# Graph attention applied ahead of its weight in a four-layer graph network kernel, with score terms as row sums and a new order on every engine

## The reference

```
h = relu(layernorm(x)); x = x + L0(h)    # 8-head masked attention, w_qkv, w_proj, + layernorm of itself
h = relu(layernorm(x)); x = x + L1(h)    # rel = (h Wq^T)(h Wk^T)^T * adj, rows scaled to norm 1, times h Wv^T
h = relu(layernorm(x)); x = x + L2(h)    # graph attention, below
h = relu(layernorm(x)); x = x + L3(h)    # adj @ h @ w_out + b_out
```

```
hw = h @ W;  s1 = hw @ a1;  s2 = hw @ a2
e = leaky_relu(s1[:, None] + s2[None, :], 0.2) * adj
att = softmax(e);  out = elu(att @ hw + beta * hw)
```

## Time and profile before

| what | value |
|---|---|
| median of 3 runs | 1475.9 us (1473.24 to 1476.55) |
| the profiled execution | 1474.6 us, its span 1472.8 us |
| TensorE (PE) busy | 1438.2 us, 98% |
| VectorE (DVE) busy | 1273.4 us, 86% |
| ScalarE (ACT) busy | 1134.7 us, 77% |
| GpSimd (POOL) busy | 748.4 us, 51% |
| mean granted TensorE clock | 0.995 of full speed |

### The profile page before, as it was taken

How to read it: one execution, slowest core, us unless ns; L and a number is a source line. 1 busy time by engine, 2 the same in 40 slices (tenths; PEclk the granted TensorE clock), 3 DMA queues, 4 the chain that set the end, 5 groups by cost and what they waited for, 6 DMA issues and landing times.

```text
span 1472.8 us, 47814 instructions
## 1 busy us (share of the span) xinstructions
PE 1438.2 (98%) x16136; PEld 1370.3 (93%) x16136; DVE 1273.4 (86%) x5774; ACT 1134.7 (77%) x2884; POOL 748.4 (51%) x1107
## 2 busy tenths in 40 slices
PE   5999999999999999999999999999999999999996
PEld 5899999999999999999999999999999999999985
DVE  4889988988989889889889889889889889889885
ACT  4778878878877877877877778778778788788753
POOL 3455555555555555555555555555555555555452
PEclk9999999999999999999999999999999999999998
DMA  3000000100000000001001000000001001000000
GB/s 111 17 17 23 31 16 30 31 16 31 30 17 31 30 16 31 28 19 31 24 23 30 23 24 30 24 24 31 23 24 30 23 24 30 19 28 31 9 23 30
DMA packets 38113, 39.90 MB, mean 27 GB/s; under 512 B 2416, under 2 KB 37488, under 8 KB 37872
## 3 DMA queue, kind: packets, MB, share of 16 engines
q1 hardware_dynamic: 37872, 36.84, 7.9%
HBM read 20.05 MB, written 16.78 MB: 25 GB/s over the span
## 4 chain that ended last, share of the span: by engine, by line
PE 95%; DVE 1%; ACT 1%; issue 1%; POOL 0%; DMA 0%; SPq 0%; POOLq 0%; ACTq 0%; DVEq 0%
PE bank L314 34%; PE mid L314 15%; PE bank L349 6%; PE mid L358 5%; PE bank L520 5%; PE bank L370 4%; PE mid L458 4%; PE mid L374 4%; PE bank L330 4%; PE mid L488 4%; PE bank L417 4%; PE mid L330 2%; PE mid L349 2%; PE mid L493 1%; PE mid L527 1%
## 5 line engine op out<-in xcount | busy, mean ns | idle before, releaser
L546 ACT ACTIVATE probs<-masked,neg_max 128x128 f32<-128x128 f32 x1024 | 326.3, 395 | 6.3 <-DVE neg_max L716 6.3
L903 POOL TENSOR_TENSOR rstd<-var_eps,minus_half 128x2 f32<-128x2 f32 x320 | 240.9, 753 | 25.5
L716 DVE CUSTOM_DVE_ANT_0 masked<-mid,mask 128x128 f32<-128x128 f32 x1024 | 234.9, 286 | 6.9 <-issue 6.8
L915 POOL TENSOR_TENSOR xb<-x,b_proj_beta 128x512 f32<-128x512 f32 x64 | 81.9, 1279 | 233.9 <-DVE o_res L828 233.9
L901 POOL TENSOR_TENSOR var_eps<-mean_var,eps 128x2 f32<-128x2 f32 x320 | 63.5, 198 | 243.0 <-DVE mean_var L710 242.7
L706 DVE BATCH_NORM_STATS2 stats<-x 128x6 f32<-128x256 f32 x384 | 143.3, 415 | 0.1
L725 DVE TENSOR_SCALAR z<-x,mean_var,rstd 128x256 f32<-128x256 f32 x384 | 134.5, 405 | 7.1 <-POOL rstd L903 6.7
L946 POOL TENSOR_TENSOR h_t_lo<-h_t_full,h_t_hi 128x512 fp32r<-128x512 f32 x64 | 82.0, 1282 | 79.4 <-ACT h_t_hi L629 79.4
L349 PE MATMUL bank<-ident,probs 128*128 128x128 f32 x768 | 117.6, 276 | 4.9 <-ACT probs L546 4.9
L942 POOL TENSOR_TENSOR e_mask<-e_leaky,adj_sb 128x256 f32<-128x256 f32 x64 | 46.8, 731 | 116.2 <-DVE e_leaky L770 116.2
L370 PE MATMUL bank<-probs_t,v 128*32 128x128 f32 x2048 | 104.5, 276 | 0.3 <-issue 0.3
(11 more groups left out here) (156 smaller groups left out, 5725.8 us busy)
## 6 DMA issues: line engine op xcount, KB each, us to landing
x<-in_x SPq DMA_DIRECT2D x64, 256.0 KB, 2.7
out_x<-x SPq DMA_DIRECT2D x64, 256.0 KB, 2.1
w_qkv_sb<-in_w_qkv SPq DMA_DIRECT2D x1, 768.0 KB, 4.4
w_q_sb<-in_w_q SPq DMA_DIRECT2D x1, 256.0 KB, 4.4
w_k_sb<-in_w_k SPq DMA_DIRECT2D x1, 256.0 KB, 4.6
w_v_sb<-in_w_v_t SPq DMA_DIRECT2D x1, 256.0 KB, 5.8
w_proj_sb<-in_w_proj SPq DMA_DIRECT2D x1, 256.0 KB, 6.0
w_gat_x<-in_w_gat SPq DMA_DIRECT2D x1, 256.0 KB, 7.2
```

The costliest lines, as they stand in the source:

```text
L546: last = act.activation(probs[:, r, s], masked[:, r, s], ACT.Exp, scale=-1.0, bias=neg_max[:, r, s:s + 1])
L716: last = dve.tensor_tensor_reduce(out=masked[:, r, s], in0=mid[:, r, s * N:(s + 1) * N], in1=mask[:], scale=1.0, scalar=LARGE, op0=ALU.add ...
L903: pool.tensor_tensor(rstd[:, k], var_eps[:, k], minus_half[:], ALU.pow).then_inc(ln_rstd[k], 1)
```

## The change

Attention is applied to the rows h2 first and the weight after: att (h2 W) = (att h2) W. In detail:
- h2 = relu(rstd * x2 - mean * rstd) is made by ScalarE straight from x2, as h3 is. z2, its four transposes, both halves of h_t2, the 258-column product, its two banks and the copies to `hw` go.
- s1 and s2 are row sums of h2 times the vectors W a1 and W a2 (`wa_rows`, spread over all partitions once, in step 3, by four transposes and a copy), four `tensor_tensor_reduce` a pair on VectorE, each over 256 elements.
- m = h2^T att_t is four f32 matmuls of 128 columns a pair. Its halves are made by ScalarE and VectorE, and u = m W is a product of 12 matmuls of 256 columns. The two f32 matmuls of the old u go.
- The leaky maximum is made by ScalarE (`Prelu` with s1 as the bias) from PSUM, in the place of `e_sum`; VectorE's instruction goes.
- z0 and z1 are made by ScalarE (`Identity` with scale rstd and bias shift) instead of VectorE; three small `shift` instructions a pair are new on VectorE.
- STREAMS becomes 10, banks are assigned anew, and the order of the blocks is new on all engines. q and k change places around the step's edge.
- At the start, the halves of w_qkv are made in three parts, behind x0's moments on VectorE; the fold moves to step 2, with its two loads behind the constants on SP's queue, and its use to step 4.

```diff
-    STREAMS = 8
+    STREAMS = 10
...
+    def wa_rows_made():
+        pe.wait_ge(wa_made, 2 * C)
+        pe.wait_ge(max_ready[0], done(1, 1))
+        for j in range(2):
+            for c in range(C):
+                last = pe.transpose(wa_bank[:, j * D + c * 128:j * D + (c + 1) * 128],
+                                    w_gat_x[:, c, D + j:D + j + 1].to_broadcast([128, 128]), ident[:])
...
-    transposes(z2_bank, z[2]).then_inc(h_t_psum[2], 1)
-    rows([hw0_bank[:, 0:DX], hw1_bank[:, 0:DX]], h_t[2], w_gat_p, 0, DX).then_inc(hw_psum, 1)
-    for b in range(2):
-        last = pe.matmul(u_bank[:, b * D:(b + 1) * D], att_t[:, b], hw[:, b, 0:D], start=True, stop=True)
+    for c in range(C):
+        for b in range(2):
+            last = pe.matmul(m_bank[:, (c * 2 + b) * N:(c * 2 + b + 1) * N], h2[:, b, c * 128:(c + 1) * 128],
+                             att_t[:, b], start=True, stop=True)
+    rows(halves(u_bank), m_t_p, w_gat_p, 0, D).then_inc(u_psum, 1)
...
-    act.activation(flat(h_t[2][0]), z2_bank, ACT.Relu).then_inc(h_hi_ready[2], 1)
-    act.activation(hw[:, b], bank[:, 0:DX], ACT.Copy).then_inc(hw_ready, 1)
-    act.activation(e_sum[:, b], s2_bank[:, b * N:(b + 1) * N], ACT.Identity, bias=hw[:, b, D:D + 1])
+    last = act.activation(h2[:, b], x2[:, i5, b], ACT.Relu, bias=shift[2][:, b:b + 1], scale=rstd[:, 2, b:b + 1])
+    last = act.activation(z[0][:, b], x0[:, i0, b], ACT.Identity, bias=shift[0][:, b:b + 1], scale=rstd[:, 0, b:b + 1])
+    last = act.activation(z[1][:, b], x1[:, i3, b], ACT.Identity, bias=shift[1][:, b:b + 1], scale=rstd[:, 1, b:b + 1])
+    act.activation(flat(m_t_p[0]), m_bank, ACT.Copy).then_inc(m_hi_ready, 1)
+    act.activation(e_leaky[:, b], s2_bank[:, b * N:(b + 1) * N], ACT.Prelu, bias=s12[:, b, 0:1], alpha=ALPHA)
...
-    normalize(1, p3, x1[:, i3])
-    normalize(0, p0, x0[:, i0])
-    normalize(2, p4, x2[:, i4])
-    dve.scalar_tensor_tensor(e_leaky[:], e_sum[:], ALPHA, e_sum[:], ALU.mult, ALU.max)
+    dve.scalar_tensor_tensor(shift[0][:], mean_var[:, 0, :, 0], -1.0, rstd[:, 0], ALU.mult, ALU.mult)\
+       .then_inc(shift_ready[0], 1)
+    last = dve.tensor_tensor_reduce(out=s12_prod[:, b, j], in0=h2[:, b], in1=wa_rows[:, j], scale=1.0, scalar=0.0,
+                                    op0=ALU.mult, op1=ALU.add, accum_out=s12[:, b, j:j + 1])
+    dve.tensor_tensor(flat(m_t_p[1]), m_bank, flat(m_t_p[0]).bitcast(f32), ALU.subtract).then_inc(m_lo_ready, 1)
```

More of the change, by code:

```diff
@@ L435, in step @@
[L435 to L445, removed]
@@ new lines, in step @@
+                if on[4]:
+                    pe.wait_ge(h_lo_ready[1], done(p4))
+                    bank_free(pe, (h1_full_ready, p4, 1), (y_lo_ready, p9, 1))
+                    columns(g_bank, w_qk_p, 0, h_t[1]).then_inc(g_psum, 1)
+                if on[1]:
+                    pe.wait_ge(h_lo_ready[0], done(p1))
+                    bank_free(pe, (x4_ready, p9, 1), (probs_t_ready[0], p2, 1))
+                    rows(halves(v_bank), h_t[0], w_qkv_p, 2 * D, D).then_inc(v0_psum, 1)
+                if on[4]:
+                    pe.wait_ge(h_lo_ready[1], done(p4))
+                    bank_free(pe, (max_ready[0], p1, 1), (x3_ready, p7, 1))
+                    rows(halves(v1_bank), h_t[1], w_v_p, 0, D).then_inc(v1_psum, 1)
@@ L469, in step @@
[L469 to L476, removed]
@@ L490, in step @@
-                if on[3]:
-                    pe.wait_ge(rel_sq_ready, done(p3))
-                    for b in range(2):
-                        last = pe.matmul(rel_bank[:, 256 + b:257 + b], rel_sq[:, b], ones[:, 0:1], start=True, stop=True)
-                    last.then_inc(sum_sq_psum, 1)
-                if on[1]:
-                    pe.wait_ge(probs_ready[1], done(p1))
-                    bank_free(pe, (h_lo_ready[0], p0, 1), (x4_ready, p7, 1), (o_norm_ready, p2, 1))
-                    transpose_probs(1).then_inc(probs_t_psum[1], 1)
@@ L522, in step @@
                     last.then_inc(y_t_psum, 1)
+                if on[2]:
+                    pe.wait_ge(o_lo_ready, done(p2))
+                    bank_free(pe, (o_norm_ready, p2, 1), (probs_t_ready[2], p2, 1))
+                    for b in range(2):
+                        last = product(o_bank[:, b * D:(b + 1) * D], o_t_p, w_proj_p,
+                                       lambda a, c: a[:, b, c], lambda a, c: a[:, c])
+                    last.then_inc(o_psum, 1)
+                if on[1]:
+                    pe.wait_ge(probs_ready[0], done(p1))
+                    bank_free(pe, (v0_ready, p1, 1), (x4_ready, p9, 1))
+                    transpose_probs(0).then_inc(probs_t_psum[0], 1)
@@ new lines, in step @@
+                if on[5]:
+                    pe.wait_ge(s12_ready, done(p5))
+                    bank_free(pe, (max_ready[2], p1, 1), (att_t_ready, p6, 1), (x2_ready, p5, 2))
+                    for b in range(2):
+                        last = pe.transpose(s2_bank[:, b * N:(b + 1) * N], s12[:, b, 1:2].to_broadcast([128, 128]), ident[:])
+                    last.then_inc(s2_psum, 1)
+                if on[6]:
+                    pe.wait_ge(m_lo_ready, done(p6))
+                    bank_free(pe, (v1_ready, p4, 1), (max_ready[0], p1, 1))
+                    rows(halves(u_bank), m_t_p, w_gat_p, 0, D).then_inc(u_psum, 1)
@@ L529, in step @@
-                    last.then_inc(s2_psum, 1)
-            run(pe, step, [(0, fold), (2, next_weights), (4, last_weights)])
+                        last = pe.matmul(rel_bank[:, 256 + b:257 + b], rel_sq[:, b], ones[:, 0:1], start=True, stop=True)
+                    last.then_inc(sum_sq_psum, 1)
+                if on[3]:
+                    if t == 3:
+                        pe.wait_ge(folded_ready, 2)
+                    pe.wait_ge(z_ready[1], done(p3))
+                    bank_free(pe, (y_lo_ready, p8, 1), (g_ready, p4, 1))
+                    transposes(z1_bank, z[1]).then_inc(h_t_psum[1], 1)
@@ new lines, in step @@
+                if on[0]:
+                    pe.wait_ge(h_lo_ready[0], done(p0))
+                    bank_free(pe, (h_lo_ready[0], p0, 1), (max_ready[1], p1, 1))
+                    columns(q_bank, w_qkv_p, 0, h_t[0]).then_inc(q_psum, 1)
+                if on[4]:
+                    pe.wait_ge(v1_ready, done(p4))
+                    pe.wait_ge(rel_ready, done(p4))
+                    bank_free(pe, (e_leaky_ready, p5, 2), (max_ready[2], p1, 1), (att_t_ready, p6, 1))
+                    for b in range(2):
+                        last = pe.matmul(rel_v_bank[:, b * D:(b + 1) * D], rel[:, b], v1[:, b], start=True, stop=True)
+                    last.then_inc(rel_v_psum, 1)
@@ L586, in step @@
-                if on[7]:
-                    act.wait_ge(shift3_ready, done(p7))
-                    wait_before(act, y_t_psum, p7)
-                    for b in range(2):
-                        last = act.activation(h3[:, b], x3_up[:, i7, b], ACT.Relu, bias=shift3[:, b:b + 1],
-                                              scale=rstd[:, 3, b:b + 1])
-                    last.then_inc(h3_ready, 1)
+                    act.wait_ge(h_t_psum[1], done(p4))
+                    wait_before(act, rel_psum, p4)
@@ L655, in step @@
                 if on[5]:
-                    act.wait_ge(att_t_psum, done(p5))
-                    wait_before(act, u_psum, p5)
-                    act.activation(att_t[:].rearrange("p b n -> p (b n)"), att_bank[:, 0:2 * N], ACT.Copy).then_inc(att_t_ready, 1)
+                    act.wait_ge(s2_psum, done(p5))
+                    wait_before(act, e_mask_ready, p5)
+                    for b in range(2):
+                        act.activation(e_leaky[:, b], s2_bank[:, b * N:(b + 1) * N], ACT.Prelu, bias=s12[:, b, 0:1], alpha=ALPHA)\
+                           .then_inc(e_leaky_ready, 1)
                 if on[1]:
@@ L738, in step @@
             def step(t, par, on):
[L739 to L745 removed]
+                p0, p1, p2, p3, p4, p5, p6, p7, p8, p9, p10 = [t - s for s in range(STREAMS + 1)]
@@ new lines, in step @@
+                if on[3]:
+                    dve.wait_ge(xb_ready, done(p3))
+                    dve.wait_ge(o_psum, done(p3))
+                    dve.tensor_tensor(o_res[:], pair_rows(o_bank), xb[:], ALU.add).then_inc(o_res_ready, 1)
+                if on[1]:
+                    relu_lo(0, p1, z0_bank)
+                if on[3]:
+                    dve.wait_ge(o_psum, done(p3))
+                    dve.tensor_tensor(o[:], pair_rows(o_bank), both(b_proj_bc), ALU.add).then_inc(o_ready, 1)
+                    dve.wait_ge(o_ready, done(p3))
+                    moments(LN_O, p3, o)
@@ new lines, in step @@
+                if on[7]:
+                    dve.wait_ge(u_exp_ready, done(p7))
+                    dve.scalar_tensor_tensor(x2_exp[:], u_exp[:], 1.0, x2[:, i7], ALU.min, ALU.add).then_inc(x2_exp_ready, 1)
+                if on[3]:
+                    dve.wait_ge(ln_moments[LN_O], done(p3, 2))
+                    for b in range(2):
```

(3 more changed lines are left out.)

667 lines of the change are left out of this document (339 added, 328 removed).

## The result

The changed kernel takes 1681.1 us (median of 4 runs, 1678.96 to 1682.04) beside 1474.8 us of the kernel before on the same chip. The ratio is 1.140 (95% interval 1.138 to 1.142). Forecast were 1443 us and a range of 1429 to 1466. Two rivals named the right side, ScalarE late for k_t (1487 us) and a table load (1511 us). Both fell short, by 194 and 170 us, and neither named the instruction that waits.

The account below looks back on a forecast made before the run. TensorE was taken to bound the kernel at 22.2 us a pair. Terms of -32 us over 64 pairs, -1.8 at the start and +2 at the end took 1474.6 to 1442.8, say 1443 us; range 1429 to 1466 (8 in 10).

Parts of the forecast that it names:

- ScalarE late for k_t: Rival: ScalarE's in-order queue makes the scores wait for k_t every step, +0.2 us a pair, 1487 us; chance 0.09.
- a table load: Rival: the leaky function is outside ScalarE's loaded table, two loads a pair, +0.6 us a pair, 1511 us; chance 0.03.
- I find no place that must stall, so I cost the new waits at nothing: Claim, from laying the engines' new orders against TensorE's prices, that the new waits between engines add 0 us.
- signs of being wrong: TensorE waits mid-kernel (scores on k_t, u on m_lo, q on h_t's low half), ScalarE above 97%, or heads above 2.1 us.
- It stays covered: VectorE goes from 19.8 to 19.6 us a pair, of a 21.7 us period, so TensorE still covers it.
- ScalarE comes to 20.2 of 21.7: ScalarE's work per pair rises from 17.7 to 20.2 us, leaving 1.5 us of slack in the 21.7 us period.
- The sum on TensorE: TensorE's change per pair: -0.44 - 0.03 + 0.02 - 0.05 = -0.50 us, ends about -0.62 and -0.25.
- z2's 0.44: TensorE's saving per pair from removing the four transposes of z2, 0.44 us.
- The joints: TensorE group costs depending on place in the order: -0.05 us a pair, ends +0.10 and -0.15.
- The low end of the sum: Most favourable end of TensorE's change per pair, about -0.62 us, or -40 us over 64 pairs.
- The ends: Fill and drain: start net -1.8 us with the first product near 11 us; end +2 us for two half-empty steps.
- some 0.6: Room in us left on ScalarE after att_t and k_t, between att_norm's transposes and the scores, called the tightest place.

Follow-up runs that it names:

- Experiments 1 and 3: 1: changed kernel with two h2 buffers, 1423.5 us; 3: changed kernel, one buffer, h2 moved behind m's high half and row sums behind its low half, 1431.9 us.
- experiments 6 to 8: Changed kernel with two h2 buffers plus one, three and two unread 128x512 copies on ScalarE between att_t and k_t: 1424.4, 1486.1 and 1451.0 us.
- experiments 2 and 4: Changed kernel, one h2 buffer; 2: z0 put ahead of h2 on ScalarE, 1625.2 us; 4: z0 and z1 back on VectorE, 1591.2 us.

## Why the prediction was wrong

- **The step that failed** is "I find no place that must stall, so I cost the new waits at nothing". It listed what each instruction reads and who waits for its result, and left out what a write must await: one h2, written for pair p in the same step in which m reads it for pair p - 1. By the prediction's own prices h2 stood on ScalarE about 5 us ahead of the end of m. The wait is in the whole diff (`wait_before(act, m_psum, p5)`), and its size could have been worked out. ln_sum waits for the heads, so h2's turn comes some 1.2 us after the scores start. From there to the end of m, the timeline of the kernel before gives 1.10 for the scores, 1.44, 1.41 and 1.49 for three products and 0.89 for m's form, 6.3 us together. Of the prediction's own signs of being wrong, two came: waits before u on m_lo and before q on the low half of h_t. Experiments 1 and 3 take the wait away in two ways, and the time falls by 258 and 249 us.
- **Price.** 25.61 - 21.38 = 4.23 us a pair against two buffers, for a term put at nothing. In the step shown it is seen on TensorE as three long distances: m to z0's transposes 3.28 for 0.89, s2's transposes to u 1.18 for 0.14, z1's transposes to q 0.95 for 0.39. They make 3.99 us. Most of the rest is in groups behind the first gap, z0's transposes 0.49 for 0.44, rel 0.98 for 0.89 and y_t 0.88 for 0.81, here at a granted clock of 1.00. Times 64 it is 271 us, the two spans differ by 257.5, since the first steps have hardly any of it.
- **"It stays covered"; "ScalarE comes to 20.2 of 21.7".** Without the wait this holds and the room was larger: ScalarE is busy for 272.40 / 300 x 21.38 = 19.4 us. Some 0.35 of the 0.8 is that instructions back to back overlap: h2 or a z takes 0.99 from start to start instead of 1.10, three times a pair. VectorE has 19.2 for a predicted 19.6.
- **The sum on TensorE, -0.50 us a pair**, was right in sign and too small: -0.82. The terms themselves held in the run with two buffers: m 719.13 - 718.24 = 0.89, the longer u 1.52, z2's 0.44 gone. The joints (what a group costs by its place in the order) were mis-sized, at -0.05 for some -0.38. y_t away from the heads takes 0.81 for 0.99, rel_v in front of transposes 0.86 for 0.96, and of three products in a row the second and third take 1.36 each for 1.41 and 1.49. Others give some of it back: o takes 1.51 for 1.42, the transposes of att_norm 0.31 for 0.22. (The low end of the sum, -0.62, is -0.60 by the prediction's own terms.) What the new order is worth apart from the smaller work was not tried.
- **The ends.** The first product was put near 11 us. It starts at 11.08 in the changed kernel. Over the span, two buffers have 1422.6 - 64 x 21.38 = 54.3 us outside the periods for 52.0 before: +2.3, predicted +0.2.
- **The rivals.** ScalarE late for k_t is a real mechanism, but was not reached: k_t had 0.77 us of room (experiments 6 to 8) where the prediction worked out some 0.6, and 0.90 - 0.14 = 0.76 in the changed kernel too. A table load did not occur: Prelu takes 367 ns for 128x128 where e_sum took 363, and there is one load at the start. The Trainium skill's rule to do `add` and `mul` on VectorE (ScalarE: Activation LUTs, Rules for kernel authors) did not decide here. With TensorE as the bound, moving z back to VectorE costs 6 us.

Even with two buffers, where its premise of no wait holds, the forecast of 1443 stands against a measured 1423.5, below its low end of 1429: -51 us instead of -32, mostly from the joints. The version with two buffers takes 3.5% less time than the kernel before, and no other version was faster.

## What to carry to other kernels

Check each new tile for its write as well as its reads: in a hand-ordered pipeline, a single buffer whose reader stands later in the same step than its next writer stops the writer's whole queue. Place the write behind the read in step order, or pay for a second buffer. Without either, the price is what the delay costs around the loop through several engines (4.23 us a pair here, for a wait of 5.07). When no engine is full and all are less busy than before, look among the longest waits for one whose releaser is a reader of the tile that the waiting instruction writes.

## What the runs showed of the hardware that I had not expected

- With two buffers, and a granted clock of 1.00, a group of 12 matmuls of 256 columns costs 1.36 to 1.52 us by its place. The first of a run costs 1.52 (u), 1.51 (o), 1.50 (q), 1.48 (g) or 1.47 (k), the second or third 1.44 (y behind k) or 1.36 (v behind g, v1 behind v). What stands ahead doesn't sort the first ones: u, q and k follow transposes, o and g f32 matmuls. What makes them differ was not tried.
- A late start of the scores cost 0.13 to 0.19 us a step beyond the lateness, in the groups behind it, at a granted clock of 1.00.
- Gaps did not always bring the clock down. With a gap of 2.23 us behind m in each step the granted clock fell for some 6 us behind every second one (0.97 over 300 us). In experiments 2 and 4, where the longest gap of a middle step is 1.3 us, it stood at 1.00 from 400 to 1400 us.
